# Two cross attentions of a perceiver kernel: output projections inside the last batch, a later context split and earlier query stores

## What is computed

```
def cross(query, context, ...):                      # layer 0; layer 1 adds a bias and a mask to the scores
    q = query @ Wq + bq
    k, v = split(context @ Wkv + bkv)
    attn = softmax(q @ k.T * scale)                  # per batch and head: 64 queries x 1024 keys
    return (attn @ v) @ Wout + bout                  # Wout: 256 x 256

x = x + cross0(layernorm(x), ctx, mask)
x = x + self0(layernorm(x))                          # attends over 16 batch entries at a position, causal, softmax with 1 + sum
x = x + experts(layernorm(x))                        # 8 experts, two for each token
x = x + cross1(layernorm(x), ctx, bias, mask)
x = x + self1(layernorm(x))                          # attends over the 64 tokens of a batch
x = x + ffn_fp4(layernorm(x))
```

## Time and profile before

| | us |
|---|---|
| median of three executions (lowest, highest) | 1399.77 (1399.67, 1403.18) |
| profiled execution | 1401.2 |
| its span | 1399.4 |
| TensorE busy, share of the span | 1249.0, 89% |
| its weight loads | 1050.5, 75% |
| VectorE | 974.2, 70% |
| ScalarE | 784.7, 56% |
| GpSimd | 636.1, 45% |
| mean granted clock of TensorE | 0.922 of full |

### The profile page before, as it was taken

One profiled execution on the slowest core, in us unless ns is written; L12 is line 12 of the kernel. 1 busy time (PEld: TensorE's weight loads), 2 busy tenths in 40 slices (PEclk: granted clock), 3 DMA queues, 4 the chain that ended last, 5 costly groups with the idle time before them and its releaser, 6 DMA issues. The chain is left out here.

```text
span 1399.4 us, 35051 instructions
## 1 busy us (share of the span) xinstructions
PE 1249.0 (89%) x12294; PEld 1050.5 (75%) x12294; DVE 974.2 (70%) x1995; ACT 784.7 (56%) x1435; POOL 636.1 (45%) x580
## 2 busy tenths in 40 slices
PE   5899999999999689529997999999999999677778
PEld 4688888888887548329995788888888887546555
DVE  5577777777777565556626777777777777478896
ACT  3577777777786211115444677777777776124211
POOL 4456656656663314033232556656656654317000
PEclk9999999999999885559998999999999999786899
DMA  6767777777765170254446686776776764100000
GB/s 203 196 178 203 176 194 191 178 194 190 178 170 137 36 61 3 87 190 146 172 153 205 174 209 179 181 206 176 182 206 176 182 177 110 36 0 3 1 4 27
DMA packets 106725, 198.33 MB, mean 142 GB/s; under 512 B 43661, under 2 KB 63790, under 8 KB 106640
## 3 DMA queue, kind: packets, MB, share of 16 engines
q1 hardware_dynamic: 105104, 193.32, 53.4%
q0 software_dynamic: 1536, 3.88, 0.8%
HBM read 88.26 MB, written 10.62 MB: 71 GB/s over the span
## 5 line engine op out<-in xcount | busy, mean ns | idle before, releaser
L845 POOL TENSOR_SCALAR cross_prob<-cross_prob,cross_inverse 128x1024 f32<-128x1024 f32 x256 | 287.6, 1124 | 348.1 <-DVE cross_inverse L595 348.1
L776 ACT ACTIVATE cross_prob<-cross_negated,cross_negmax 128x1024 f32<-128x1024 f32 x256 | 295.0, 1152 | 134.6 <-DVE cross_negmax L587 134.4
L587 DVE CUSTOM_DVE_ANT_0 cross_negated<-cross_scores,cross_bias 128x1024 f32<-128x1024 f32 x256 | 313.5, 1225 | 25.4 <-PE cross_scores L483 7.2
L496 PE MATMUL cross_turn<-ident,cross_prob 128*128 128x128 f32 x2048 | 273.0, 276 | 16.3 <-POOL cross_prob L845 8.9
L496 PEld LDWEIGHTS cross_turn<-ident,cross_prob 128*128 128x128 f32 x2048 | 241.7, 142 | 57.2 <-POOL cross_prob L845 13.0
L785 ACT COPY cross_probT<-cross_turn 128x512 f32<-128x512 f32 x256 | 149.4, 583 | 65.7 <-PE cross_turn L496 64.6
L603 DVE COPY cross_probT<-cross_turn 128x512 f32<-128x512 f32 x256 | 175.6, 686 | 5.3 <-PE cross_turn L496 5.3
L483 PE MATMUL cross_scores<-cross_keys,cross_qbd 96*128 96x512 f32 x512 | 170.4, 414 | 1.7 <-POOL cross_qbd L837 1.7
L825 POOL TENSOR_TENSOR cross_ctx_lo<-cross_raw,cross_ctx_hi 128x512 fp32r<-128x512 f32 x120 | 155.8, 1300 | 10.2 <-ACT cross_ctx_hi L752 10.2
L426 PE MATMUL cross_out<-cross_wv_hi,cross_ctx_lo 128*128 128x256 f32 x488 | 147.9, 303 | 0.0
L428 PE MATMUL cross_out<-cross_wv_hi,cross_ctx_hi 128*128 128x256 f32 x488 | 137.8, 282 | 0.0
(11 more groups left out here) (275 smaller groups left out, 2134.4 us busy)
## 6 DMA issues: line engine op xcount, KB each, us to landing
cross_keys<-cross_key_hi SPq DMA_DIRECT2D x512, 128.0 KB, 2.4
cross_raw<-in_ctxT SPq DMA_DIRECT2D x32, 1024.0 KB, 5.6
cross_keys<-cross_key_lo SPq DMA_DIRECT2D x256, 128.0 KB, 2.4
cross_bias<-bias_rows SPq DMA_DIRECT2D x32, 512.0 KB, 3.7
up_sb<-in_moe_w SPq DMA_DIRECT2D x8, 1024.0 KB, 8.8
down_sb<-in_moe_w SPq DMA_DIRECT2D x8, 1024.0 KB, 5.7
cross_stacked_q<-q_rows SPq DMA_DIRECT2D x90, 64.0 KB, 2.0
q_rows<-cross_negated SPq DMA_DIRECT2D x8, 256.0 KB, 2.2
```

The source lines that it names most:

```text
L496: last = pe.transpose(ps_t[part][:, k * P:(k + 1) * P], prob[n % 2][:, kt * P:(kt + 1) * P], ident)
L587: dve.tensor_tensor_reduce(negated[n % 2], ps_s[n % 2][:, :], bias_sb[par][:, :], -1.0, 3.0e38, ALU.add, ALU.min, negmax[:, n % 2:n % 2 + ...
L776: act.activation(prob[n % 2][:, :], negated[n % 2], ACT.Exp, bias=negmax[:, n % 2:n % 2 + 1], scale=-1.0, accum_out=total[:, n % 2:n % 2 + ...
L845: pool.tensor_scalar(prob[n % 2][:, :], prob[n % 2][:, :], inverse[:, n % 2:n % 2 + 1], 1.0, ALU.mult, ALU.mult).then_inc(prob_ready, 1)
```

## The change

1. Each cross attention makes the output projections of tiles 0 to 6 itself, in its last batch (`project_out`): tiles 0 and 1 at pairs 2 and 4, 2 and 3 behind the turn of pair 5, 4 and 5 behind the turns of pairs 6 and 7, 6 behind the last weighing. GpSimd adds the bias behind each divide of that batch. VectorE joins tile i to `x` and takes its statistics (`join`): 0 and 1 ahead of the copies of turns 6 and 7, 2 and 3 ahead of copy_out, 4 to 6 behind it. `project_block` keeps tile 7, and the wait for the weights goes into the next block, `normalize_block`.
2. At the start of each cross attention GpSimd waits until all eight tiles are normalised before it splits the context of batch 1; in cross attention 0 the first spread stands behind two of the splits, in cross attention 1 ahead of all four.
3. There SP issues the last two query stores ahead of more of the key transfers.
4. Both self attentions spread the queries three tiles ahead. Self attention 1 adds all eight biases behind the first three spreads, and projects one iteration later (i = 8 and 9).

```diff
--- before.py
+++ after.py
@@ -83,6 +83,11 @@
         stat_step, rooted, normed = sem("stat_step"), sem("rooted"), sem("normed")
         turned, copied = sem("turned"), sem("copied")
         block = ctx.enter_context(nc.Block())
+
+        if loaded is not None:
+            @block.sync
+            def _(sp):
+                sp.wait_ge(*loaded)
 
         @block.vector
         def _(dve):
...
@@ -240,6 +245,8 @@
         turn_ready, turn_copied_a, turn_copied_v = sem("turn_ready"), sem("turn_copied_a"), sem("turn_copied_v")
         half_weighed = sem("half_weighed")
         pv_done, half_ready, out_copied = sem("pv_done"), sem("half_ready"), sem("out_copied")
+        projected, biased, joined, seen_out = sem("projected"), sem("biased"), sem("joined"), sem("seen_out")
+        y_banks = [ps_p[:, 0:D], ps_p[:, D:2 * D]] + [ps_s[i][:, at:at + D] for i in range(2) for at in (0, 512)] + [ps_s[0][:, D:2 * D]]
         if start is not None:
             away, at_key = (sb(n, [B, S2], U8) for n in ("away", "at_key"))
             row0, row1, side = first.negated[0:B, 0, :], first.negated[0:B, 1, :], prob[1][0:B, :]
@@ -384,12 +391,15 @@
             load_ctx(2)
             sp.wait_ge(qbd_ready, G)
             load_queries(1)
-            for n in range(ahead + 2, 6):
+            if taken is not None:
+                first_keys(5)
+                first_keys(6)
+            store_queries(2, q_stored)
+            if taken is None:
+                first_keys(4)
+            store_queries(3, q_stored)
+            for n in range(5 if taken is None else 7, PAIRS):
                 first_keys(n)
-            store_queries(2, q_stored)
-            first_keys(6)
-            store_queries(3, q_stored)
-            first_keys(7)
             first.load_out(sp)
             sp.wait_ge(q_stored, 32 * (len(q_jobs) - G))
 
@@ -550,6 +560,21 @@
                 project_value(0, 0, piece)
             turn_tokens(1)
 
+            def project_out(i):
+
+                pe.wait_ge(first.wo_loaded, 16)
+                pe.wait_ge(out_copied, 4 * i + 4)
+                if i < 2:
+                    pe.wait_ge(key_lo_done, 4 * B)
+                else:
+                    pe.wait_ge(max_ready, 8 * B - (1 if i < 4 else 0))
+                if i == 6:
+                    pe.wait_ge(joined, 3)
+                for k in range(G):
+                    last = pe.matmul(y_banks[i], oT[:, k, i * P:(i + 1) * P], first.wo[:, k, :],
+                                     start=(k == 0), stop=(k == G - 1))
+                last.then_inc(projected, 1)
+
             def body(b, par):
                 for n in range(8):
                     scores(b, par, n)
@@ -557,14 +582,21 @@
                         project_queries(G + n)
                     two_before(turn, b, n)
                     project_at(b, par, n, project_key, project_value)
+                    if in_last(b, 1) and n in (2, 4):
+                        project_out(n // 2 - 1)
                     if n == 5:
                         weigh(b, par, 0)
                     if n == 1 and not is_first(b):
                         weigh(b - 1, 1 - par, 1)
             batches(pe, body)
-            for n in (6, 7):
-                turn(B - 1, n)
+            project_out(2)
+            project_out(3)
+            turn(B - 1, 6)
+            project_out(4)
+            turn(B - 1, 7)
+            project_out(5)
             weigh(B - 1, 1, 1)
+            project_out(6)
 
         @block.vector
         def _(dve):
@@ -734,11 +766,27 @@
                         split_queries(G + n)
                     two_before(copy_turn, b, n)
                     taken_at(b, par, n, rest_key, lambda b, par, piece: None)
+            def join(i):
+
+                dve.wait_ge(projected, max(i + 1, 2))
+                dve.wait_ge(biased, i + 1)
+                dve.tensor_tensor(x[:, i, :], x[:, i, :], y_banks[i], ALU.add).then_inc(joined, 1)
+                dve.wait_ge(joined, i + 1)
+                dve.bn_stats(stats[:, i, :], x[:, i, :]).then_inc(seen_out, 1)
+                dve.wait_ge(seen_out, 2 * i + 1)
+                dve.bn_aggr(moments_out[:, i, :], stats[:, i, :]).then_inc(seen_out, 1)
+
             batches(dve, body)
             invert(B - 1, 7)
-            for n in (6, 7):
-                copy_turn(B - 1, n)
+            join(0)
+            copy_turn(B - 1, 6)
+            join(1)
+            copy_turn(B - 1, 7)
+            join(2)
+            join(3)
             copy_out(B - 1, 1)
+            for i in range(4, NT - 1):
+                join(i)
 
         @block.scalar
         def _(act):
@@ -862,15 +910,11 @@
             root(1)
             if start is not None:
                 pool.wait_ge(ident_loaded, 32)
-                for piece in range(4):
-                    split_lo(1, 1, piece)
-                spread(0, 0, 0)
-            else:
-                for piece in range(2):
-                    split_lo(1, 1, piece)
-                spread(0, 0, 0)
-                for piece in range(2, 4):
-                    split_lo(1, 1, piece)
+            pool.wait_ge(normed, NT)
+            for piece in range(4):
+                if piece == (0 if start is None else 2):
+                    spread(0, 0, 0)
+                split_lo(1, 1, piece)
             spread(0, 0, 1)
 
             def body(b, par):
@@ -880,50 +924,43 @@
                         spread(b + 1, 1 - par, SPREAD_STEPS.index(n))
                     if n in split_steps(b) and not in_last(b, 2):
                         split_lo(b + 2, par, split_steps(b).index(n))
+                    if in_last(b, 1):
+                        pool.tensor_tensor(x[:, n, :], x[:, n, :], first.bo[:, :], ALU.add).then_inc(biased, 1)
             batches(pool, body)
 
 
-def project_block(nc, tag, aT, w, b_row, x, moments, loads):
...
+def project_block(nc, tag, aT, w, x, moments, loads, loaded):
...
         @block.sync
         def _(sp):
             for out, in_ in loads:
                 sp.dma_start(out, in_).then_inc(loaded, 16)
-            sp.wait_ge(loaded, 16 * len(loads))
-
-        @block.gpsimd
-        def _(pool):
-            for i in range(NT):
-                pool.tensor_tensor(x[:, i, :], x[:, i, :], b_row, ALU.add).then_inc(biased, 1)
...
+            for k in range(G):
+                last = pe.matmul(ps[:, :], aT[:, k, i * P:(i + 1) * P], w[:, k, :], start=(k == 0), stop=(k == G - 1))
+            last.then_inc(ready, 1)
...
+            dve.wait_ge(ready, 1)
+            dve.tensor_tensor(x[:, i, :], x[:, i, :], ps[:, :], ALU.add).then_inc(added, 1)
...
@@ -1137,8 +1174,8 @@
                     turn(i - 2)
                 if i >= 3:
                     weigh(i - 3)
-                if ahead is not None and NT - 1 <= i < NT + 1:
-                    for tile in (2 * (i - NT + 1), 2 * (i - NT + 1) + 1):
+                if ahead is not None and NT <= i < NT + 2:
+                    for tile in (2 * (i - NT), 2 * (i - NT) + 1):
                         project(tile)
 
         @block.vector
@@ -1302,15 +1339,16 @@
                 pool.wait_ge(stat_step, pair + 2)
                 pool.tensor_tensor(ahead.rstd[:, at], ahead.shifted[:, at], ahead.half_power[:, at], ALU.pow).then_inc(rooted, 1)
 
-            spread_queries(0)
-            spread_queries(1)
+            for i in range(3):
+                spread_queries(i)
+            if ahead is not None:
+                for i in range(NT):
+                    bias(i)
             for i in range(NT):
-                if i + 2 < NT:
-                    spread_queries(i + 2)
+                if i + 3 < NT:
+                    spread_queries(i + 3)
                 if ahead is None or i < NT - 1:
                     divide(i)
-                if ahead is not None:
-                    bias(i)
             if ahead is not None:
                 for pair in range(2):
                     root(pair)
...
```

40 lines of the change are left out of this document (16 added, 24 removed).

## The result

| | before | changed |
|---|---|---|
| median of the timed executions, us | 1399.80 (1399.67 to 1403.18, 4 runs) | 1383.47 (1382.24 to 1384.67, 4 runs) |
| profiled execution, its span | 1401.2, 1399.4 | 1382.8, 1381.0 |

The ratio is 0.9884, 95% interval 0.9862 to 0.9906: the change makes the kernel 16.3 us faster. The forecast was 14.3 us (1385.5).

The account below looks back on a forecast made before the run. TensorE was taken to bound the loops, and chains of waits through several engines the ends, starts and self attentions. Gains 8.7 + 4.5 - 1.2 + 2.7 - 0.4 = 14.3 us gave 1385.5 us; 8-in-10 range 1378 to 1394.

Parts of the forecast that it names:

- Tails: Ends of both cross attentions: projections inside the last batch gain 8.7 us, the middle of 6.5 to 11.0.
- 1.14 us for tile 7's projection: Tail of cross attention 0: 1.14 us to the add of tile 7, in a stretch summed to 7.7 us.
- Start of cross attention 0: Later GpSimd split, earlier query stores and a shorter low clock gain 4.5 us, bounds 3.4 and 6.5.
- 0.9 us that VectorE's subtraction gains: Start of cross attention 0: subtraction without GpSimd's split beside it takes 0.69 us, not 1.67, so 0.9 us earlier.
- 3.3 for the queue: Start of cross attention 0: six fewer 128 KB key transfers ahead of the last query store give 3.3 us.
- Start of cross attention 1: Earlier scores are lost in ScalarE's longer store wait, TensorE cold behind it: loss 1.2 us, bounds 4.0 gained, 3.0 lost.
- Self attention 0: Spreading queries three tiles ahead removes four TensorE waits: gain 2.7 us, bounds 1.5 and 2.7.
- Self attention 1: Tile 7's 1.76 us score wait goes, projection pairs come later: loss 0.4 us, bounds 1.8 gained, 2.5 lost.
- E: Rival, slower: GpSimd's 24 bias adds hold VectorE, 16.6 us lost, 1402.1 us or up to 1413; chance 5%.
- D: Rival: last-batch projections are not hidden, costing 12.5 us over both cross attentions, 1398 us; chance 5%.
- C: Rival, cold: tails 6.5, starts 3.4 and -3.0, self attentions 1.5 and -1.5, gain 6.9, 1392.9 us; chance 20%.
- B: Rival, warm: full clock in tails (11.0), starts 6.5 and 0, self attentions 2.7 and 1.0, 1378.6 us; chance 15%.

Follow-up runs that it names:

- second profile: The changed kernel, unedited, run again on another chip: median 1381.26 us, ratio 0.9865 to the kernel before.
- e4: Changed kernel with the start of cross attention 1 as before on GpSimd and SP: median 1380.97 us, ratio 0.9856 to the kernel before.
- e8: Changed kernel with cross attention 1's query stores ahead of two pairs' key transfers and self attention 1's projection pairs one iteration earlier: median 1376.12 us, ratio 0.9820.
- e7: Changed kernel with projections 2 to 5 behind the last weighing and joins 2 and 3 behind the copy of its result: median 1389.24 us, ratio 0.9912.
- e1: Changed kernel with parts 2 to 4 undone, leaving only the tails' projections, biases and joins: median 1388.05 us, ratio 0.9901 to the kernel before.
- e2: Changed kernel with GpSimd's order at both cross attention starts as before, SP's store order new: median 1382.07 us, ratio 0.9858 to the kernel before.
- e6: Changed kernel with cross attention 1's query stores issued ahead of the key transfers of pairs 5 and 6: median 1381.51 us, ratio 0.9866.
- e5: Changed kernel with self attention 1's projection pairs in iterations 7 and 8, as before: median 1382.07 us, ratio 0.9875 to the kernel before.

## Why the prediction was right, step by step

The forecast was 14.3 us, in the parts 8.7, 4.5, -1.2, 2.7 and -0.4. The medians give 16.3, 2.0 more. The stages of the second profile add up to 16.5, and there the 2 us more are in the tails and self attention 1, with some 1.1 us each. Measured by stages in the two profiles of the changed kernel:

- **Tails, 8.7:** 9.8 and 9.9 (3.6 + 6.2, 3.9 + 6.0). From the last accumulate on, the sum of rows held within 0.1 us in cross attention 1 and was 0.9 too good in cross attention 0. The step that failed there is the 1.14 us for tile 7's projection, which runs at the low clock behind the change of blocks (2.09). Where it came out as forecast (the kernel run again, and e4) the tail was only 0.3 to 0.5 shorter, since SP's issues of the five loads then ended last, which the sum did not have. The agreement in cross attention 1 has some luck in it, since that projection took 1.47 us in this profile and 2.04 in e8. The question left open was the clock in the tail itself: it stays full, as the windows show and e7 by taking the fill away. So the forecast's 8.7 was the middle between two clocks of which only the full one came; that one was priced at 11.0, and 0.9 of the 1.2 missing to it is this block of cross attention 0.
- **Start of cross attention 0, 4.5:** 7.1 and 4.4, and 3.3 to 5.2 in the eight other kernels whose stores are early, so the size is right and the first profile's 7.1 is its own; 1.4 of the 2.7 between the two is the step behind the context load of the third batch. But one step of its sum failed: the 0.9 us that VectorE's subtraction gains when GpSimd splits later. The subtraction did shrink (0.69), and normalisations end early (VectorE, then GpSimd, after):

```profile
30.78 1.38 DVE L695 TENSOR_SCALAR cross_probT<-x,cross_moments,cross_rstd 128x256 f32<-128x256 f32 x4
...
38.02 1.23 DVE L619 CUSTOM_DVE_ANT_0 cross_negated<-cross_scores,cross_bias 128x1024 f32<-128x1024 f32 x1 [5.85 <-PE cross_scores L493]
...
35.94 1.04 POOL L885 TENSOR_TENSOR cross_qbd<-cross_stacked_q,half_mask 96x512 fp32r<-96x512 f32 x1 [1.11 <-DMA cross_stacked_q<-q_rows]
```

  What was late next had not been named: the first spread waits for the reload of the queries (1.11 us), and the first maxima start at 38.02, against 38.83. Over all profiles they start at 38.02 to 40.22 in the ten with the later split there, and at 38.81 to 40.19 in the three without it (before, e1, e2): no order in it. The other step, 3.3 for the queue, held: ScalarE's copy started at 54.79 or 54.80 in the three kernels with the old stores and at 49.8 to 52.0 in the others, 2.8 to 5.0 earlier.
- **Start of cross attention 1, -1.2:** -1.5 in both. The mechanism is the forecast's to the letter: a wait grown to 4.2 us that ends within 0.1 us of its old place, with a cold TensorE behind it. The prediction put it on the context load ahead of the store; e6 shows that the key transfers ahead of it count too, and can go: the wait ended 1.7 us sooner for three transfers. The section "Queues, rings and completion order" of the Trainium skill's page "DMA: Bandwidth & Descriptors" says that descriptors are consumed in the order of the ring on each engine, and both fit that.
- **Self attention 0, 2.7:** 3.0 in each of the eleven profiles with the part, 0.1 worse than before without it (e1).
- **Self attention 1, -0.4:** +0.7, so the sign was wrong. e5 parts the sum in two: the later projections lose 2.3 us, about what the forecast had (the second pair ends right at the last weighing, and its joins start beside it and end behind it), and the rest gains 3.0, not the 1.76 counted. The forecast had only the wait of tile 7's scores there, which shrank to 0.88 us and did not go. The rest of the 3.0 is in the tiles ahead of it: the starts of the scores of tiles 2 to 7 stood 5.12, 4.68, 5.13, 4.92 and 4.88 us apart in before and stand 4.67, 4.67, 4.80, 3.81 and 3.81 apart in the changed kernel, in which every spread is made one tile earlier and no bias add stands between the divides.
- **Rivals.** E, that the bias adds hold VectorE, did not show: maxima of 1.22 to 1.23 and steps of 2.69 in the last batch, with a GpSimd busier by 0.73 us in each step. That is what the Trainium skill's page "SBUF — State Buffer", "Who interferes with whom", says of an instruction with one SBUF input. D fell with the unchanged step. Of C's open links, start 1 and self 1 both came out better than it had them, and its cold tails did not come. B had the clock of the tails right and the rest too high; its 1378.6 is 4.9 us below the first median and 2.7 below the second.

## What to carry over

Work put into idle time of TensorE was worth twice in these tails: once for itself, and once because the full clock lasted through the gap (e7). When one of two things that end at nearly the same time is sped up, expect nothing until the other goes too, and look in the queue ahead of the waited-for transfer for what can stand behind it. Behind it a third may wait, here a context load two batches on. Price by stage borders, and profile one kernel twice before trusting a difference below 3 us in a stage that waits for transfers or in which the clock rises.

## What the runs showed of the hardware

- Stages with the same code differ from one execution to the next in steps. The norm and rotary stage ahead of self attention 0 is 2.0 us shorter in seven of the thirteen profiles than in the others (within 0.2 us, but for e2's 0.6 more). In the seven the granted clock of TensorE is back at 1.00 some 1.3 to 2.2 us ahead of the first rotary projection, in the other six only 3.6 to 5.7 us behind its start. Its first four products took 3.75 us in the kernel before and 1.96 in e1, with the same code (before, then e1):

```profile
488.91 3.75 PE L973 MATMUL self_rope_qk_ps<-self_w,self_xnT 128*128 128x512 f32 x4 [1.35 <-PEq L78]
```

```profile
487.85 1.96 PE L1019 MATMUL self_rope_qk_ps<-self_w,self_xnT 128*128 128x512 f32 x4 [1.69 <-PEq L78]
```

- One wait length and two outcomes: behind 1.76 us of idle time TensorE went on at the full clock in the kernel before (granted 1.00 from 1284 to 1296), behind 1.74 us in e1 the granted clock fell to 0.50 for some 10 us (1274 to 1284).
- In the change of blocks inside a tail TensorE is idle for 3.61 us (cross attention 0) or 4.15 us (1), in e7 for 2.61 and 3.15, and the projection of tile 7 behind it took 1.10 to 2.05 us in the twelve profiles with the change: in cross attention 0 it took 1.10 in the changed kernel run again and 2.05 the first time. In the slow case the granted clock was 0.50 beside it.
- GpSimd's 256-column add takes 0.73 us beside VectorE's maxima and 0.69 beside its joins; neither makes the other longer by more than 0.04.
